# A macaron layer on one core: four products summed by one instruction a step, and attention's weights inverted on 128 partitions by way of DRAM

## The chip, the cores and the metric

The kernel runs on one core of a Trainium2 chip. The metric is the device time of one execution in microseconds (us). TensorE (PE), VectorE (DVE), ScalarE (ACT) and GpSimd (POOL) compute; SyncE (SP) and POOL issue the DMAs here. Each engine works through its own list in order and waits on semaphores, so a wait holds up everything behind it on that engine.

## What is computed

Everything is float32. The input is 4 batches of 512 tokens of width 512. A layer is feed-forward, attention, feed-forward, each added to the stream after a row normalisation:

```
x = x + 0.5 * ffn(layernorm(x))
x = x + attention(layernorm(x))
x = x + 0.5 * ffn(layernorm(x))
ffn: top 2 of 8 experts (512 -> 256 -> 512, gelu) + a shared pair 512 -> 512 -> 512
attention (K=32 heads, H=8 columns, M=8 frequencies):
  z = causal conv of 4 taps over x @ W_mem;  q = x @ W_q
  p = exp(log weight), one row of 512 per head
  num(t) = cumsum over t of p * cos(k*theta_m), p * sin(k*theta_m)
  den(t) = cumsum of p;  out = sum over m of num * q / max(den, 1e-4)
  gated by silu, then @ W_out
```

The kernel scans `run(t) = run(t-1) * p(t-1)/p(t) + cos` (and the same with sin), which is num(t)/p(t); so it needs the **falls** p(t-1)/p(t) inside the scan and the **fractions** p(t)/den(t) afterwards.

## The kernel before, in words

All five lists are written out at build time by a planner. `piece(engine, stage, cost, *after)` declares a stage with an assumed duration and what it comes after; `orders()` then fills each engine in turn with the open piece of longest remaining way. Attention's vector pieces are put behind all others that are open. So a changed cost or dependency moves pieces on every engine, far from the edited code.

**Feed-forward.** Jobs q = 0 to 7 (batches 0 to 3, twice). A job loads rows (`fetch`), normalises, turns them (L710), computes logits (L719), the shared hidden layer (L736) and its second product (L748), added to DRAM by POOL. Two jobs make a group g; its token pairs are sorted by expert into 23 blocks, each: rows gathered by POOL (L1538), turned (L780), two products with the expert's weights (L789, L805), and one accumulating scatter (L1551). The 23 scatters of a group run one after another, because each may hit rows of the one before.

**Attention.** It starts for batches 0 and 1 when group 0 is done, for 2 and 3 when group 1 is done. Per batch: three conv inputs and four query products on PE (L824, L833), queries stored to DRAM (`q_cols<-xin`, L1689), the convolution and log weights on DVE, the exponential on ACT (L1030). Then DVE works out falls and fractions on the 32 partitions that hold one head each: `falls` (L1304, L1306) and `denominators` (L1312 to L1318). PE spreads falls to 128 partitions by a product with 0/1 rows (L840) and ACT keeps the result in `pwx` (L1037); PE spreads the fractions (L846) when they are used.

Then 16 **steps** per batch, 64 in all: 2 halves of the heads by 8 frequencies m. A step loads its queries into `qx` (SP, L1704, two DMAs), makes phases (DVE, L1330 and L1332), cos and sin (ACT, L1043 to L1046), scans (L1343, twice), multiplies real and imaginary parts (L1350, L1355), and adds: two instructions join the two halves of each product (L1366, L1368), and from m = 1 on two more add these to `outT` (L1374, L1376). `trig` and `qx` have two slots, so a step's phases and queries wait for the sums of the step before last. After 8 steps `scale_output` (L1388) multiplies by the fractions, SP moves the result to `outT` (L1710), PE, ACT and DVE apply the gate (L858, L1056, L1400), PE makes the output rows (L867) and POOL adds them to the stream. Only then can the second feed-forward job of that batch fetch its rows.

Of the kernel before, what the change touches and what calls it, by code (L numbers as in the profile page):

```python
# [15 lines left out]
P = 128  # L16
# [45 lines left out]
def macaron(nc, x, small, gate_w, sw1, sw2, b2_rows, w_experts, w_mem, w_q, w_bd, w_out, out):  # L62
# [32 lines left out]
    with ctx:  # L95
# [13 lines left out]
        pw, logw_sb = (low_rows[0:K, :, :], low_rows[2 * K:3 * K, :, :]), low_rows[K:2 * K, 0, :]  # L109
        w_all = sb("w_all", [P, E * WE])  # L110
# [55 lines left out]
        cmp_a = sb("cmp_a", [P, TB, E, E])  # L166
        cmp_b = sb("cmp_b", [P, TB, E, E])
# [20 lines left out]
        past = cmp_a.rearrange("p t e f -> p (t e f)")[:, 0:NB * E].rearrange("p (j e) -> p j e", e=E)  # L188
        is_of = cmp_b.rearrange("p t e f -> p (t e f)")[:, 0:NB * E].rearrange("p (j e) -> p j e", e=E)
        of_bias = past  # L190
# [5 lines left out]
        NK = 2 * HALVES  # L196
        kval = sb("kval", [P, NK, T])
        pwx = sb("pwx", [P, HALVES, T])
        outT = sb("outT", [P, HALVES, 2, T])
        NQX = 2  # L200
        qx = sb("qx", [P, NQX, 2, T])

        trig = sb("trig", [P, 2, 2, T])
        trig_int = trig.bitcast(I32)
        run = sb("run", [P, 2, T])[:, :, :]
# [26 lines left out]
        q_dram = nc.dram_tensor("q_cols", (2, KQ, M, HH, 2, T), F32)  # L232
        slots_dram = [nc.dram_tensor(f"slots{g}", (P * NB, 2), F32).ap() for g in range(NG)]
# [141 lines left out]
        def plan_head(b):  # L375
# [14 lines left out]
            for i in (HALVES, *range(HALVES)):  # L390
                s = ("a_mem", b, i)
                free = [("DVE", ("c_turn", b - 2, i * M + M - 1))] if i < HALVES and b >= 2 else []
                free += [("DVE", ("a_den", b - 1))] if i == HALVES and b else []
# [4 lines left out]
                  *([("PE", ("c_out", b - 2, HALVES - 1)), ("PE", ("a_spread", b - 2, HALVES - 1))] if b >= 2 else []))  # L398
# [8 lines left out]
            for half in range(HALVES):  # L407
                s = ("a_spread", b, half)
                piece("PE", s, 1.2, ("DVE", ("a_fall", b)),
                      *([("DVE", ("c_scan", b - 1, half * M + M - 1))] if b else []), bank=[("misc", ("ACT", s))])  # L410
                piece("ACT", s, 0.6, ("PE", s))

        def plan_step(i):
# [6 lines left out]
            piece("DVE", ("c_scan", b, n), 2.5, ("ACT", ("c_turn", b, n)), ("ACT", ("a_spread", b, half)),  # L420
# [489 lines left out]
        def scalar_program():  # L910
# [121 lines left out]
            def keep_falls(b, half):  # L1032
                bank = misc_turn.at["a_spread", b, half][0]
                act.wait_ge(*spread_p.at((b, half)))
                if b > 0:
                    act.wait_ge(*scanned.at((b - 1, half * M + M - 1)))
# [827 lines left out]
```

## Time and profile before

| | |
|---|---|
| median of 3 runs | 1300.2 us (1297.55 to 1307.3) |
| the profiled execution: its own time, its span | 1298.54 us, 1297.3 us |
| mean granted TensorE clock | 0.894 of full speed |
| busy: PE, DVE, ACT, POOL | 1018.4, 718.9, 586.2, 447.5 us |
| DMA issued on SP, on POOL | 93.58 MB, 60.90 MB |

No engine is busy throughout, and the shares are averages over stages. Up to 243 us DVE has almost nothing to do (expert group 0); from 290 to 1031 us it is busy 80% of the time with attention, beside the expert groups 1 and 2; after 1031 us it is idle again. Durations of DVE instructions in these rows overlap by up to 0.08 us where one does not depend on the other, so a sum of busy time is not the time that a sequence takes: the distance between two starts is.

### The profile page before, as it was taken

What the parts mean: (1) busy time and instruction counts of PE and PEld (TensorE: products, weight loads), DVE (VectorE), ACT (ScalarE), POOL (GpSimd) and SP (SyncE); (2) the same over time, 40 slices, a digit from 0 to 9 for tenths busy, and PEclk for the clock granted to TensorE, in tenths of its full rate; (3) what the DMA queues carried; (4) which work ended last, traced back from release to release, by engine and by line L of the source; (5) the groups of instructions that cost most, each with busy time, mean ns of one, the idle gap of its engine ahead of it and who ended that gap; (6) DMA issues with size and microseconds to landing.
All of it is one profiled execution on the core that took longest, in us unless ns stands there. A gap on an engine that the chain in (4) does not pass through costs nothing.

```text
span 1297.3 us, 10733 instructions
## 1 busy us (share of the span) xinstructions
PE 1018.4 (78%) x3296; PEld 562.8 (43%) x3296; DVE 718.9 (55%) x1162; ACT 586.2 (45%) x1003; POOL 447.5 (34%) x428
## 2 busy tenths in 40 slices
PE   6999779972969869969946379877976897979884
PEld 3547545422525435445412144344443543546552
DVE  4311000077779979979998978889977810200000
ACT  4324333323415768567423254268475741214332
POOL 4164443202453343332000227144354212244442
PEclk9999998995878979988987779889988999789888
DMA  8955554424154656675333742367775525035554
GB/s 299 373 155 97 99 89 74 78 61 137 27 105 109 165 118 138 134 211 148 83 99 77 198 113 51 81 177 147 147 209 121 80 36 108 30 73 96 94 92 53
DMA packets 60204, 155.15 MB, mean 120 GB/s; under 512 B 10578, under 2 KB 10578, under 8 KB 57974
## 3 DMA queue, kind: packets, MB, share of 16 engines
q0 software_dynamic: 29568, 60.90, 27.7%
q1 hardware_dynamic: 30582, 93.58, 23.9%
q8 instruction: 28, 0.46, 0.2%
q14 instruction: 26, 0.21, 0.1%
HBM read 99.74 MB, written 58.88 MB: 122 GB/s over the span
## 4 chain that ended last, share of the span: by engine, by line
DMA 37%; PE 25%; DVE 15%; POOL 8%; ACT 7%; issue 7%; SPq 1%; POOLq 0%; ACTq 0%; DVEq 0%
DMA out_rows<-ys,into_i 14%; DMA x_rows<-ys,into_i 12%; PE hps L736 5%; POOL slots L1526 4%; PE misc L867 4%; DMA xs<-x_normal,rows_i 3%; PE yps L748 3%; DVE run L1343 3%; DMA xin<-x_rows 2%; PE yps L805 2%; PE xps L719 2%; ACT ys L975 2%; PE hps L789 2%; PE misc L833 2%; DVE trig L1350 1%
## 5 line engine op out<-in xcount | busy, mean ns | idle before, releaser
L805 PE MATMUL yps<-w_all,hidden_sb 128*128 x368 | 194.5, 656 | 47.8 <-ACT hidden_sb L962 47.2
L789 PE MATMUL hps<-w_all,hidden_sb 128*128 x736 | 182.4, 393 | 4.0 <-ACT hidden_sb L945 4.0
L789 PEld LDWEIGHTS hps<-w_all,hidden_sb 128*128 128x128 f32 x736 | 143.0, 200 | 47.8 <-issue 31.2
L1343 DVE TENSOR_TENSOR_SCAN run<-pwx,trig 128x512 f32<-128x512 f32 x128 | 149.4, 1208 | 24.0 <-ACT trig L1046 23.4
L1538 POOL DMA_INDIRECT xs<-x_normal,rows_i x92 | 106.9, 1162 | 109.3 <-PE xps L780 82.1
L1551 POOL DMA_INDIRECT x_rows<-ys,into_i x46 | 82.7, 1797 | 158.3 <-DMA x_rows<-ys,into_i 84.9
L736 PE MATMUL hps<-xnT,sw_sb 128*128 128x512 f32 x256 | 130.8, 666 | 7.5 <-ACT hidden_sb L935 6.8
L975 ACT ACTIVATE ys<-yps,slots 128x512 f32<-128x512 f32 x92 | 62.9, 685 | 160.5 <-DMA out_rows<-ys,into_i 61.6
L1551 POOL DMA_INDIRECT out_rows<-ys,into_i x46 | 81.0, 1761 | 152.3 <-DMA out_rows<-ys,into_i 76.3
L805 PEld LDWEIGHTS yps<-w_all,hidden_sb 128*128 128x128 f32 x368 | 70.4, 203 | 117.5 <-issue 115.6
L748 PE MATMUL yps<-sw_sb,hidden_sb 128*128 128x512 f32 x256 | 118.4, 605 | 0.0
L780 PE MATMUL xps<-ident,xs 128*128 128x128 f32 x368 | 58.2, 288 | 69.3 <-DMA xs<-x_normal,rows_i 66.9
L1526 POOL DMA_INDIRECT slots<-told,dest_i x64 | 74.3, 1161 | 72.3 <-DVE cmp_a L1213 30.8
L867 PE MATMUL misc<-turns_sb,tail_sb 128*128 128x512 f32 x192 | 88.6, 615 | 7.6 <-DVE tail_sb L1404 7.6
L710 PE MATMUL xps<-ident,xin 128*128 128x128 f32 x128 | 26.1, 360 | 76.7 <-ACT xin L996 71.1
L736 PEld LDWEIGHTS hps<-xnT,sw_sb 128*128 128x128 f32 x256 | 53.7, 215 | 73.8 <-issue 66.1
L780 PEld LDWEIGHTS xps<-ident,xs 128*128 128x128 f32 x368 | 44.2, 146 | 87.1 <-DMA xs<-x_normal,rows_i 63.2
L1259 DVE BATCH_NORM_STATS2 stats_attn<-xin 128x6 f32<-128x512 f32 x16 | 10.5, 688 | 127.7 <-DMA xin<-x_rows 127.6
L1350 DVE TENSOR_TENSOR trig<-run,qx 128x1024 f32<-128x1024 f32 x64 | 77.9, 1218 | 4.0 <-DMA qx<-q_cols 3.6
L1355 DVE TENSOR_TENSOR qx<-run,qx 128x1024 f32<-128x1024 f32 x64 | 77.9, 1217 | 0.0
L1043 ACT ACTIVATE trig<-trig 128x512 f32<-128x512 f32 x64 | 40.4, 631 | 74.1 <-DVE trig L1332 74.0
L748 PEld LDWEIGHTS yps<-sw_sb,hidden_sb 128*128 128x128 f32 x256 | 46.0, 189 | 53.7 <-issue 53.7
(193 smaller groups left out, 1570.8 us busy)
## 6 DMA issues: line engine op xcount, KB each, us to landing
qx<-q_cols SPq DMA_DIRECT2D x128, 256.0 KB
x_normal<-xin SPq DMA_DIRECT2D x32, 256.0 KB, 3.2
w_all<-in_w_experts SPq DMA_DIRECT2D x8, 1024.0 KB, 9.0
xin<-x_rows SPq DMA_DIRECT2D x32, 256.0 KB, 6.6
turns_sb<-in_w_out SPq DMA_DIRECT2D x3, 1536.0 KB, 10.4
xin<-in_x SPq DMA_DIRECT2D x16, 256.0 KB, 3.6
x_rows<-ys POOLq DMA_DIRECT2D x16, 256.0 KB, 4.6
q_cols<-xin SPq DMA_DIRECT2D x16, 256.0 KB
```

The lines of the kernel that those rows point to most:

```text
L736: t = PE.matmul(hps[:, bank, :], sw1_sb[:, c, n * P:(n + 1) * P], xnT[:, c, :], start=c == 0, stop=c == KC - 1)
L748: t = PE.matmul(yps[:, bank, :], hT[:, n, tb * P:(tb + 1) * P], sw2_sb[:, n, :], start=False, stop=n == SC - 1)
L780: t = PE.transpose(xps[:, bank, c * P:(c + 1) * P], xs[:, j % NX, c * P:(c + 1) * P], ident[:, :])
L789: t = PE.matmul(hps[:, bank, 0:H], xT[:, j % 2, c, :], w_all[:, bass.ds(expert[j] + c * H, H)], start=c == 0, stop=c == KC - 1)
L805: t = PE.matmul(yps[:, bank, :], hb[:, j % 2, ec, :], w_all[:, bass.ds(expert[j] + (KC * H + ec * D), D)], start=ec == 0, stop=ec == EC - 1)
L867: t = PE.matmul(misc[:, bank, :], yT[:, v, tb * P:(tb + 1) * P], wout_sb[:, v, :], start=v == 0, stop=v == VT - 1)
L975: SE.activation(ys[:, j % 2, :], yps[:, bank, :], ACT.Copy, scale=slots[:, g % 2, j, 1:2]).then_inc(*ys_kept.of((g, j)))
L1343: t = VE.tensor_tensor_scan(run[:, c, :], pwx[:, n // M, :], trig[:, n % 2, c, :], 0.0, ALU.mult, ALU.add)
L1350: VE.tensor_tensor(trig[:, n % 2, :, :], run[:, :, :], qx[:, n % NQX, :, :], ALU.mult).then_inc(*real_made.of((b, n)))
L1526: GE.indirect_dma_start(slots_dram[g], bass.IndirectOffsetOnAxis(dest_i[:, g % 2, t, r:r + 1], 0), told[:, g % 2, t, r, :], None).then_inc ...
L1538: GE.indirect_dma_start(xs[:, j % NX, :], None, xn_rows[g % 2], bass.IndirectOffsetOnAxis(rows_i[:, g % 2, j:j + 1], 0)).then_inc(*xs_load ...
L1551: GE.indirect_dma_start(INTO[g], bass.IndirectOffsetOnAxis(into_i[:, g % 2, j:j + 1], 0), ys[:, j % 2, :], None, compute_op=ALU.add).then_ ...
```

## The change

**Sums.** One tile `sums` [128, 2, 2, 512] holds all four sums (two products for the real and two for the imaginary part). `trig` and `qx` become two planes of one tile `steps_sb`, so one instruction over 2048 elements adds all four products. A step with m = 0 writes its products straight into `sums`, and must wait until the previous half has been scaled. The two halves of each part are joined once per half, after m = 7. `outT` loses its dimension for the half; the number of kept conv tiles falls from 4 to 3; `cmp_a` and `cmp_b` shrink.

**Weights.** p is stored to DRAM (one element into the tensor) and read back twice as 128 rows of 128, once as it is and once shifted by one: reciprocal and product then run over 128 elements instead of 512. Falls go to DRAM and are read back with each row repeated 8 times, straight into `pwx`: no product on PE and no copy on ACT. The running sum of p stays on 32 partitions, goes to DRAM, comes back as 128 x 128, and the fractions return the same way. Per batch that is ten DMAs on SP's queue. The planner's costs and dependencies follow.

```diff
-            piece("DVE", ("a_fall", b), 4.0, ("ACT", ("a_p", b)))
-            piece("DVE", ("a_den", b), 5.8, ("DVE", ("a_fall", b)))
+            piece("SP", ("a_p", b, 0), 0.5, ("ACT", ("a_p", b)))
+            piece("SP", ("a_p", b, 1), 0.9, ("SP", ("a_p", b, 0), 2.4), *([("DVE", ("a_frac", b - 1))] if b else []))
+            piece("DVE", ("a_fall", b), 1.4, ("SP", ("a_p", b, 1), 2.4))
+            piece("SP", ("a_den", b, 1), 0.5, ("SP", ("a_den", b, 0), 2.4))
+            piece("DVE", ("a_frac", b), 1.8, ("SP", ("a_den", b, 1), 2.4), ("SP", ("a_p", b, 1), 2.4))
...
-            piece("DVE", ("c_sum", b, n), 2.8 if m else 1.4, ("DVE", ("c_times", b, n)),
-                  *([] if m or not b else [("PE", ("o_gate", b - 1, half * VH + VH - 1))]))
+            piece("DVE", ("c_sum", b, n), 0.1 if m == 0 else 2.4 if m < M - 1 else 3.8, ("DVE", ("c_times", b, n)))
...
             def falls(b):
-                p, fall = pw[b % 2][:, 0, :], pw[b % 2][:, 1, :]
-                vec.wait_ge(*p_made.at(b))
-                VE.reciprocal(fall, p).then_inc(*falling.of((b, 0)))
+                vec.wait_ge(*u_loaded.at((b, 1)))
+                VE.reciprocal(den_q, u_q).then_inc(*falling.of((b, 0)))
                 vec.wait_ge(*falling.at((b, 0)))
-                VE.tensor_tensor(fall[:, 1:T], p[:, 0:T - 1], fall[:, 1:T], ALU.mult).then_inc(*falling.of((b, 1)))
+                VE.tensor_tensor(fall_q, fall_q, den_q, ALU.mult).then_inc(*falling.of((b, 1)))
...
+            def sum_products(b, n):
+                vec.wait_ge(*real_made.at((b, n)))
+                vec.wait_ge(*imag_made.at((b, n)))
+                if n % M > 1:
+                    vec.wait_ge(*summed.at((b, n - 1)))
+                VE.tensor_tensor(sums[:, :, :, :], sums[:, :, :, :], steps_sb[:, :, n % 2, :, :],
+                                 ALU.add).then_inc(*summed.of((b, n)))
...
+            def move_sums(b, part):
+                if part == 0:
+                    sp.wait_ge(*den_made.at(b))
+                    SP.dma_start(whole_rows(den_dram[b % 2]), s_row).then_inc(*den_stored.of(b))
+                else:
+                    sp.wait_ge(*den_stored.at(b))
+                    sp.wait_ge(*falling.at((b, 1)))
+                    SP.dma_start(den_q, quarters(den_dram[b % 2])).then_inc(*den_loaded.of(b))
```

**How the lists move, at three places.** SP, batch 0, from the first query store on. Before (`qx` are the step's queries, the L1661 rows fetch the next job):

```order
L1689 DMA q_cols<-xin 2x64x512 [waits s_qT] x2
L1704 DMA qx<-q_cols 64x1x1024 [waits s_q_stored1,s_q_stored0]
L1704 DMA qx<-q_cols 64x1x1024 x3
L1689 DMA q_cols<-xin 2x64x512 [waits s_qT] x2
L1661 DMA xin<-in_x 128x512 x2
```

Now (`weights` is p in DRAM, `quarter_rows` the tile of 128 x 128 pieces; the four L1784 rows are the same query loads):

```order
L1784 DMA steps_sb<-q_cols 64x1x1024 [waits s_q_stored1,s_q_stored0]
L1784 DMA steps_sb<-q_cols 64x1x1024
L1725 DMA weights<-low_rows 32x512 [waits s_p]
L1784 DMA steps_sb<-q_cols 64x1x1024 x2
L1732 DMA quarter_rows<-weights 128x128 [waits s_before_first,s_u_stored]
L1733 DMA quarter_rows<-weights 128x128
L1756 DMA sums<-low_rows 32x512 [waits s_den]
L1716 DMA q_cols<-xin 2x64x512 [waits s_qT]
L1760 DMA quarter_rows<-sums 128x128 [waits s_falling,s_den_stored]
L1740 DMA falls<-quarter_rows 128x128
L1749 DMA pwx<-falls 128x1x512 [waits s_falls_stored]
```

The exponential's store stands behind the wait for two query stores, and the third query store stands ahead of the falls' store.

DVE, batch 1, around the falls and fractions. Before (the L1274 and L1277 rows are the convolution of the next tile):

```order
L1355 TENSOR_TENSOR qx<-run,qx 128x1024
L1304 RECIPROCAL low_rows<-low_rows 32x512 [waits s_p]
L1306 TENSOR_TENSOR low_rows<-low_rows 32x511 [waits s_falling]
L1274 TENSOR_SCALAR kval<-misc,small_sb 128x512 [waits s_mem]
L1277 SCALAR_TENSOR_TENSOR kval<-misc,small_sb,kval 128x511 [waits s_convolved]
L1277 SCALAR_TENSOR_TENSOR kval<-misc,small_sb,kval 128x510 [waits s_convolved]
L1277 SCALAR_TENSOR_TENSOR kval<-misc,small_sb,kval 128x509 [waits s_convolved]
L1312 SCALAR_TENSOR_TENSOR low_rows<-low_rows,zero 32x512
L1314 TENSOR_SCALAR low_rows<-low_rows 32x512 [waits s_den]
L1316 RECIPROCAL low_rows<-low_rows 32x512 [waits s_den]
```

Now:

```order
L1337 SCALAR_TENSOR_TENSOR low_rows<-low_rows,zero 32x512 [waits s_p]
L1368 SCALAR_TENSOR_TENSOR run<-pwx,steps_sb 128x512 [waits s_imag,s_trig]
L1368 SCALAR_TENSOR_TENSOR run<-pwx,steps_sb 128x512
L1391 TENSOR_TENSOR sums<-sums,steps_sb 128x2048 [waits s_real]
L1329 RECIPROCAL quarter_rows<-quarter_rows 128x128 [waits s_falls_stored,s_u_loaded]
L1331 TENSOR_TENSOR quarter_rows<-quarter_rows 128x128 [waits s_falling]
L1342 TENSOR_SCALAR quarter_rows<-quarter_rows 128x128 [waits s_den_loaded]
```

The load that L1342 waits for is issued by SP only after L1331 has ended (the wait on `falling` in `move_sums`), and nothing stands between the two.

PE, from the end of expert group 2 to the turning of the last job's rows. Before (L867 are the output rows of batch 3, six instructions each; L748 the shared product of job 6):

```order
L867 MATMUL misc<-turns_sb,tail_sb 128x512 x6
L746 MATMUL yps<-bias_parts 128x512
L748 MATMUL yps<-sw_sb,hidden_sb 128x512 x4
L867 MATMUL misc<-turns_sb,tail_sb 128x512 x6
L746 MATMUL yps<-bias_parts 128x512
L748 MATMUL yps<-sw_sb,hidden_sb 128x512 x4
L710 MATMUL xps<-ident,xin 128x128 x16
```

Now, the end of the blocks (L846 is a block's second product, L893 a gate product, its first pair here that of batch 3's second half; L751 turns a tile of rows):

```order
L893 MATMUL misc<-outT,wbd_sb 128x512
L893 MATMUL xps<-outT,wbd_sb 128x512
L846 ISA
L846 MATMUL yps<-w_all,hidden_sb 128x512
L846 ISA
L846 MATMUL yps<-w_all,hidden_sb 128x512
```

and the same place as before, the end of the output rows (L902; L789 is the shared product, L751 the turning):

```order
L902 MATMUL misc<-turns_sb,tail_sb 128x512 x6
L787 MATMUL yps<-bias_parts 128x512
L789 MATMUL yps<-sw_sb,hidden_sb 128x512 x4
L787 MATMUL yps<-bias_parts 128x512
L789 MATMUL yps<-sw_sb,hidden_sb 128x512 x4
L787 MATMUL yps<-bias_parts 128x512
L789 MATMUL yps<-sw_sb,hidden_sb 128x512 x4
L787 MATMUL yps<-bias_parts 128x512
L789 MATMUL yps<-sw_sb,hidden_sb 128x512 x4
L751 MATMUL xps<-ident,xin 128x128 x16
```

The first gate pair of batch 3's second half now stands ahead of the last block's product, where it stood behind the logits, and all four shared products of job 6 stand behind the last output rows, where three of them stood ahead of these.

## Rows read from the trace of the kernel before

**Rows 1.** Busy time by stretch; columns: stretch, length, PE, PEld, DVE, ACT, POOL, PEclk, DMA share, GB/s.

```profile
1031.00:1090.00 59.00, 59.00 (x159) 27.30 (x158) 8.98 (x32) 20.41 (x25) 8.72 (x9) 0.97 0.40 63
```

**Rows 2.** Groups of DVE instructions by form: busy us, mean ns of one, then idle before.

```profile
L1149 DVE RECIPROCAL gr<-diff 128x4 f32<-128x4 f32 x8 | 1.4, 178 | 0.3
L1199 DVE TENSOR_TENSOR pair<-sel,dest 128x128 f32<-128x128 f32 x4 | 1.2, 292 | 0.1
```

**Rows 3.** DVE in order of time, one step: start us, us, what.

```profile
628.46 1.22 DVE L1355 TENSOR_TENSOR qx<-run,qx 128x1024 f32<-128x1024 f32 x1
629.60 0.68 DVE L1366 TENSOR_TENSOR trig<-trig 128x512 f32<-128x512 f32 x1
...
632.01 2.33 DVE L1343 TENSOR_TENSOR_SCAN run<-pwx,trig 128x512 f32<-128x512 f32 x2
```

**Rows 4.** DVE in order of time, batch 0's weights and first steps.

```profile
275.69 3.33 DVE L1304 RECIPROCAL low_rows<-low_rows 32x512 f32<-32x512 f32 x1
279.06 0.68 DVE L1306 TENSOR_TENSOR low_rows<-low_rows 32x511 f32<-32x511 f32 x1
...
283.97 1.21 DVE L1312 TENSOR_TENSOR_SCAN low_rows<-low_rows,zero 32x512 f32<-32x512 f32 x1
...
289.76 2.34 DVE L1343 TENSOR_TENSOR_SCAN run<-pwx,trig 128x512 f32<-128x512 f32 x2
...
299.34 2.73 DVE L1110 BATCH_NORM_STATS2 stats_ffn<-xin 128x6 f32<-128x512 f32 x4 [3.81 <-DMA xin<-in_x]
...
305.81 1.22 DVE L1350 TENSOR_TENSOR trig<-run,qx 128x1024 f32<-128x1024 f32 x1
```

**Rows 5.** ACT in order of time, batch 0's exponential.

```profile
271.90 0.63 ACT L1030 ACTIVATE low_rows<-low_rows 32x512 f32<-32x512 f32 x1 [0.78 <-DVE low_rows L1297]
```

**Rows 6.** SP's queue in order of time, batch 0: query store, then loads that waited for it.

```profile
269.85 0.54 SPq L1689 DMA_DIRECT2D q_cols<-xin  x1
277.89 2.53 SPq L1704 DMA_DIRECT2D qx<-q_cols  x4
```

**Rows 7.** The tile outT: its moves, SBUF to SBUF, 64 rows of 2 KB.

```profile
DMA to landing us min/median/max: 2.3/2.4/3.3
```

**Rows 8.** Chain of waits in order of time, one such move at 503 us.

```profile
503.29 5.08 DMA outT<-tail_sb
```

**Rows 9.** Page part 6, a load on SP: count, KB each, us to landing.

```profile
xin<-in_x SPq DMA_DIRECT2D x16, 256.0 KB, 3.6
```

**Rows 10.** DVE in order of time, the end of attention's last half.

```profile
1030.24 1.41 DVE L1388 SCALAR_TENSOR_TENSOR tail_sb<-outT,small_sb,misc 128x512 f32<-128x512 f32 x2
```

**Rows 11.** SP's queue in order of time, the four moves behind it.

```profile
1031.68 2.91 SPq L1710 DMA_DIRECT2D outT<-tail_sb  x4
```

**Rows 12.** PE in order of time: last gates, output rows, job 6's shared product, job 7.

```profile
1031.23 3.63 PE L719 MATMUL xps<-gate_sb,xnT 128*128 128x8 f32 x32
...
1045.08 1.02 PE L858 MATMUL misc<-outT,wbd_sb 128*128 128x512 f32 x2
...
1046.80 3.60 PE L736 MATMUL hps<-xnT,sw_sb 128*128 128x512 f32 x8
...
1083.42 5.31 PE L867 MATMUL misc<-turns_sb,tail_sb 128*128 128x512 f32 x12
...
1089.08 3.70 PE L748 MATMUL yps<-sw_sb,hidden_sb 128*128 128x512 f32 x8
1101.71 1.97 PE L710 MATMUL xps<-ident,xin 128*128 128x128 f32 x8 [8.92 <-ACT xin L996]
```

**Rows 13.** POOL in order of time: first and last scatter of groups 2 and 3, 23 each.

```profile
859.02 1.79 POOL L1551 DMA_INDIRECT out_rows<-ys,into_i  x1 [2.73 <-ACT ys L975]
...
1039.90 1.54 POOL L1551 DMA_INDIRECT out_rows<-ys,into_i  x1 [3.79 <-DMA out_rows<-ys,into_i]
...
1168.18 1.63 POOL L1551 DMA_INDIRECT out_rows<-ys,into_i  x1 [2.31 <-ACT ys L975]
...
1292.45 1.55 POOL L1551 DMA_INDIRECT out_rows<-ys,into_i  x1 [3.92 <-DMA out_rows<-ys,into_i]
```

More of the change, by code:

```diff
@@ L109, in macaron @@
         pw, logw_sb = (low_rows[0:K, :, :], low_rows[2 * K:3 * K, :, :]), low_rows[K:2 * K, 0, :]
+        quarter_rows = sb("quarter_rows", [P, 3, T // 4])
+        u_q, fall_q, den_q = [quarter_rows[:, i, :] for i in range(3)]
         w_all = sb("w_all", [P, E * WE])
@@ L232, in macaron, with quarters, whole_rows @@
         q_dram = nc.dram_tensor("q_cols", (2, KQ, M, HH, 2, T), F32)
+        u_dram = [nc.dram_tensor(f"weights{i}", (K * T + 1, 1), F32).ap() for i in range(2)]
+        falls_dram = [nc.dram_tensor(f"falls{i}", (K, T), F32).ap() for i in range(2)]
+        den_dram = [nc.dram_tensor(f"sums{i}", (K, T), F32).ap() for i in range(2)]
+        part_dram = [nc.dram_tensor(f"fractions{i}", (K, T), F32).ap() for i in range(2)]
+        def quarters(dram, start=0):
+            return bass.AP(dram.tensor, dram.offset + start, [[T // 4, P], [1, T // 4]])
+        def whole_rows(dram, start=0):
+            return bass.AP(dram.tensor, dram.offset + start, [[T, K], [1, T]])
         slots_dram = [nc.dram_tensor(f"slots{g}", (P * NB, 2), F32).ap() for g in range(NG)]
@@ L408, in plan_head @@
                 s = ("a_spread", b, half)
-                piece("PE", s, 1.2, ("DVE", ("a_fall", b)),
-                      *([("DVE", ("c_scan", b - 1, half * M + M - 1))] if b else []), bank=[("misc", ("ACT", s))])
-                piece("ACT", s, 0.6, ("PE", s))
+                piece("SP", s, 0.5, ("SP", ("a_fall", b), 2.4),
+                      *([("DVE", ("c_scan", b - 1, half * M + M - 1))] if b else []))
         def plan_step(i):
@@ L1347, in real_products @@
             def real_products(b, n):
+                into = trig[:, n % 2, :, :] if n % M else sums[:, 0, :, :]
                 vec.wait_ge(*scanned.at((b, n)))
                 vec.wait_ge(*q_loaded[n % NQX].at((b, n, QH - 1)))
-                VE.tensor_tensor(trig[:, n % 2, :, :], run[:, :, :], qx[:, n % NQX, :, :],
-                                 ALU.mult).then_inc(*real_made.of((b, n)))
+                if n % M == 0 and STEPS_OF.index((b, n)) >= M:
+                    vec.wait_ge(*out_scaled.at(half_before(b, n)))
@@ L1468, in vector_program @@
                     denominators(*at)
+                elif stage == "a_frac":
+                    fractions(*at)
                 elif stage == "c_turn":
@@ new lines, in store_falls, with spread_falls @@
+            def store_falls(b):
+                sp.wait_ge(*falling.at((b, 1)))
+                if b >= 2:
+                    for half in range(HALVES):
+                        sp.wait_ge(*falls_loaded[half].at(b - 2))
+                SP.dma_start(quarters(falls_dram[b % 2]), fall_q).then_inc(*falls_stored.of(b))
+            def spread_falls(b, half):
+                sp.wait_ge(*falls_stored.at(b))
+                if b > 0:
+                    sp.wait_ge(*scanned.at((b - 1, half * M + M - 1)))
+                src = bass.AP(falls_dram[b % 2].tensor, falls_dram[b % 2].offset + half * KT * T,
+                              [[T, KT], [0, HH], [1, T]])
+                SP.dma_start(pwx[:, half, :], src).then_inc(*falls_loaded[half].of(b))
@@ L1757, in sync_program @@
                         SP.dma_start(x1_rows[i][GR:GR + P, :], xs[:, i, :]).then_inc(*cleared.of(NG + 2 * i + 1))
+                    for i in range(2):
+                        SP.dma_start(u_dram[i][0:1, :], xs[0:1, i, 0:1]).then_inc(*before_first.of(i))
                 elif stage == "w_head":
```

213 lines of the change are left out of this document (123 added, 90 removed).

## The prediction

> **What bounds the kernel now.** I read the busy shares first, then the chain of waits, then DVE, PE and SP in order of time. Three stretches follow one another. Up to 243 us the expert blocks of group 0 run alone; the change adds a few DMAs there and nothing else. From 290 to 1031 us DVE works through 64 steps of attention and is never long without work. From there to 1090 us PE is busy for all of 59.00 us [rows 1]: logits and hidden layer of job 6, gates and output rows of batch 3, job 6's shared products. After 8.92 us of idleness it turns job 7's rows at 1101.71 us [rows 12]; then come job 7 and the last 23 scatters, the last at 1292.45 us [rows 13]. The change touches nothing after 1101.71 us, so its worth is how much earlier that turning starts. Two things hold it: the end of attention's last scaling, at 1030.24 + 1.41 = 1031.65 us [rows 10], and the end of group 2's blocks on PE, at about 1031.2 us, where the logits start [rows 12].
>
> **From these two ends to the end of the kernel.** By the new PE list the first gate pair comes 5.3 us after the last scaling (2.91 us of issues [rows 11], 2.4 us to land [rows 7]). Behind it: three gate pairs of 1.7 (1046.80 - 1045.08), a block's product and a turn, 2.5 (an estimate from such instructions' 0.5 us each, half of the 1.02 a pair), four hidden tiles of 3.5, logits 3.5, four output rows of 5.2, a small turn 0.5, four shared products of 4.1 (3.70 and the bias product ahead of it) [rows 12]. That is 5.3 + 5.1 + 2.5 + 14.0 + 3.5 + 20.8 + 0.5 + 16.4 = 68.1 us after the scaling, 1099.7 us if it did not move: **2.0 us gained by order alone**, since the shared products now cover the time in which job 7's rows are fetched and normalised (13 us from the last output row to the turning, less than the 16.4). If attention is not the last, PE goes on from the blocks' end with two gate pairs, 0.5, 14.0, 3.5, 20.8, 0.5 and 16.4: 59.1 us, or 1090.3 us, so **at most 11.4 us** unless the blocks end earlier too.
>
> **Sums.** Four additions take from 629.60 to 632.01 us, 2.41 us, though each lasts 0.68 [rows 3]: they do not depend on one another and overlap. From 512 to 1024 elements an instruction grows from 0.68 to 1.22 us, so 2048 should last 0.68 + 3 x 0.535 = 2.29. But it waits for the product just before it, which ends at 628.46 + 1.22 = 629.68, and a dependent instruction starts 0.04 later (279.06 behind 275.69 + 3.33 [rows 4]); it would end at 632.01, and the next start 0.08 earlier: 0.08 a step, not 0.45. Times 56: 4.5 us. The m = 0 steps lose two additions (8 x 1.2 = 9.6), the joining after m = 7 adds two and a dependence (8 x 1.32 = 10.6). **Net 3.5 us**; between 0 and 11, the latter if another piece stands between product and sum each time. The new wait of a m = 0 step on the scaling stands right behind it in DVE's own list and costs nothing while that one does not wait.
>
> A rule speaks for more. The Trainium skill ("VectorE: DVE Perf Modes", The DRAIN you can't avoid) says that the next operation does not start before the pipe is empty and that only the count of operations matters; by it each of the 56 steps gives 0.45 us, 25 in all. The starts in [rows 3] lie 2.41 apart over four operations of 0.68, so this trace does not agree.
>
> **Weights on DVE.** Before, a batch spends 4.05 us on falls (3.33, one product of 0.68, 0.04) and 289.76 - 283.97 = 5.79 on sums and fractions [rows 3, 4]. A reciprocal grows from 0.178 us at 4 elements to 3.33 at 512 [rows 2, 4], 6.2 ns an element, so 0.95 at 128; other operations on 128 x 128 take 0.29 [rows 2]. Falls: 0.95 + 0.29 + 0.08 = 1.32; running sum 1.25; fractions 0.29 + 0.95 + 0.29 + 0.12 = 1.65. 4.2 for 9.8: **5.6 us a batch** before waits. PE's two small products and ACT's two copies a batch go too; neither engine is waited for there, so I put that at nothing.
>
> **Waits.** The falls now need a store and two loads after the exponential, on SP about 0.55 + 2.4 + 1.1 + 2.4 = 6.5 us at the landing of [rows 7], and a store and a load of 256 KB, 3.0 + 4.2 [rows 7, 9], before the scan. Nothing of this is in the trace of before; a landing lies between 2.4 [rows 7] and 5.1 us [rows 8]. I take 2.4, the same size of move, but later where a query store is ahead: one issued at 269.85 lets the loads behind it go only at 277.89, so it takes 7.5 us [rows 6]. The Trainium skill ("DMA: Bandwidth & Descriptors", Rules for kernel authors) says that an outermost dimension below 16 confines a DMA to that many engines, and this store's is 2; a small transfer on 16 engines would then wait behind it on two.
>
> - Batch 0. The exponential is done at 272.5 [rows 5], but the store waits for SP until 279.1 (two query loads after 277.89). Loads land at 286.5, falls end at 287.8, their store lands with the third query store at 292, the spread load at 296. The first scan starts 6.4 us later than 289.76. But phases and fractions are then done, two scans and products follow at once, and before, DVE stood 3.81 us for job 3's rows [rows 4]; the second step's products come at about 304.7 instead of 305.81. **Gain 1.1**, between -6 and 5.
> - Batch 1. The wait for the exponential stays. Behind it a query store goes out just ahead of the loads, so they land 9.5 us after the exponential, with 5.8 us of work in between: 4 us of wait. The load for the fractions is issued only after the falls and follows at once in DVE's list: 0.5 + 2.4 = 2.9. **5.6 - 6.9 = -1.3**, between -10 and 3.
> - Batches 2 and 3 have 8 us of other work ahead of the falls and 3 to 5 ahead of the fractions; I leave 1 us of wait: **4.6 each**, between -4 and 5.6.
>
> **The sum.** Attention's end: 3.5 + 1.1 - 1.3 + 9.2 = 12.5 us earlier, which by order gives 14.5. Group 2 starts after batch 1's output rows, so its blocks end earlier only by half the sums and the first two batches: 1.7 + 1.1 - 1.3 = 1.5, which gives 11.4 + 1.5 = **12.9**, the smaller. 1298.5 - 12.9 = 1285.6 us for the profiled execution; that one lies 1.7 us below the median of the runs shown, so **1287 us**.
>
> **Rivals.** A measurement of this kernel tells about 1% (13 us) from no change: its three runs lie 10 us apart.
> - *As forecast*, 1281 to 1292 us: 0.37, on both sides of 1% (1287), 0.23 of it faster.
> - *The blocks shorten too*, 1272 us: group 2's 22 gaps between scatters take (1039.90 - 859.02) / 22 = 8.2 us, group 3's, alone, 5.65 [rows 13]. Attention's pieces now stand earlier among the blocks. If a quarter of that 56 us goes, 14 more, less what attention then lacks. For: DVE is 12 us ahead. Against: the blocks wait for ACT, PE and DMA in turn. 0.22.
> - *Joined sums at their full 0.45 us*: attention 33 us earlier, blocks 12, so 1298.5 - 23.5, 1277 us by the median. 0.04; it is the rule above.
> - *The gain stops at the blocks*: batch 1 loses more than it gains, the blocks end 5 us later, 11.4 - 5 = 6.4 left: 1294 us. For: all waits priced at the quiet landing. 0.22.
> - *Slower: SP's list becomes the wait.* Each batch's ten DMAs stand in one list with the queries' loads, and six are followed by a wait for landing. At 5.1 us a landing (2.7 more each for store, load, store, spread) and a query store of 7.5 ahead, a batch loses up to 18 us of start, of which cover takes half. In three batches it eats the 20.3 us saved and the 2.0 of order from 7.4 us each; at 12 each it makes the kernel 13.7 slower: 1314 us. For: the 5.1 is from where batch 0 ends. Against: before, query stores already stood in that list ahead of loads [rows 6], and DVE kept its pace. 0.13.
> - *The wide addition does not do it*: were 2048 elements slower than twice a 1024 one (2.44), 8 us go: 1295 us. 0.02.
>
> Faster by over 1%: 0.23 + 0.22 + 0.04 = 0.49. Within 1%: 0.14 + 0.22 + 0.02 = 0.38. Slower: 0.13. The range, 1264 to 1307 us, takes in the blocks' rival with half as much again and the milder half of the slower one.
>
> **What the new trace would show.** The 2048 additions at 2.3 us, starting 0.04 after the product; DVE busy down by about 49 us (25 for sums, 23 for weights), four times what attention gains. The first scan near 296 us. In batch 1 a wait on u of about 4 and on the sums of about 3 us. The last scaling near 1019 us, the blocks' end near 1030, and PE without the gap of 8.92 us before job 7. I am wrong if a query load makes DVE wait, if the fractions' wait exceeds 5 us, or if the end of the blocks moves by over 8 us either way.

## The result and the profile after

The changed kernel is **slower: 1339.5 us** (median of four, 1326.6 to 1348.9) against 1303.6; the ratio is 1.026, 95% interval [1.021, 1.031]. I had forecast 1287 us and a range to 1307. The profiled execution (1348.88 us, span 1347.6) is the slowest of the four and counts as a slow run, which the ratio leaves out. Its span is 50.3 us over that of before, where the ratio says 34 us, so lengths read from it overstate the loss. 8.6 us of it are lost at the start: the rows of batch 0's attention arrive at 248.59 us, against 240.00 before; in `move_first` below, the same kernel but for the place of one load in SP's list, they arrive at 237.73. Further kernels are compared by ratio to the kernel before on the same chip, since chips differ by up to 9 us.

On the whole page VectorE was busy for 718.9 us before, and is for 689.7 now:

```profile
PE 1029.4 (76%) x3280; PEld 570.2 (42%) x3280; DVE 689.7 (51%) x994; ACT 584.6 (43%) x997; POOL 462.7 (34%) x428
...
L1391 DVE TENSOR_TENSOR sums<-sums,steps_sb 128x2048 f32<-128x2048 f32 x56 | 128.2, 2289 | 4.2
```

So VectorE did get its work off, and the wide addition lasts what was forecast. Now from the first scan to the last scaling, VectorE alone (stretch, length, busy, TensorE clock, DMA share, GB/s); before the same stretch was 742.60 us with 644.83 busy:

```profile
307.01:1068.63 761.62, 620.29 (x735) 0.84 0.52 124
```

24.5 us less work, 19.0 us more time: the waits in it grew from 97.8 to 141.3 us. The attention's end moved by 36.3 us: 8.6 from the early part, 8.6 from the later first scan, 19.0 here. The same stretch of `move_first`, profiled in an execution of 1330.8 us, has the same work and is 14 us shorter, 5.0 us longer than before:

```profile
298.81:1046.44 747.63, 620.73 (x735) 0.86 0.54 127
```

Which waits (`after`, VectorE between 285 and 1100 us; total, times, longest):

```profile
DVE tail_sb L1424 <- ACT tail_sb L1082: 52.1, 8, 16.8
DVE run L1368 <- ACT steps_sb L1072: 20.5, 10, 5.8
DVE quarter_rows L1329 <- DMA quarter_rows<-weights: 20.3, 3, 10.3
DVE quarter_rows L1342 <- DMA quarter_rows<-sums: 11.0, 4, 4.4
DVE steps_sb L1379 <- DMA steps_sb<-q_cols: 10.9, 3, 5.2
```

31.3 us are the weights' own round trips. The first row, 25.0 us before, is the multiplications with the output gates. This window reaches past both ends of the stretch. Its longest wait for the gates, 16.77 us, comes behind the last scaling, and 10.27 us of the wait on the weights come ahead of the first scan:

```profile
1084.69 0.69 DVE L1424 TENSOR_TENSOR tail_sb<-misc,tail_sb 128x512 f32<-128x512 f32 x1 [16.77 <-ACT tail_sb L1082]
```

Inside the stretch the gates' row reads, before and now:

```profile
DVE tail_sb L1400 <- ACT tail_sb L1056: 15.7, 6, 6.9
```

```profile
DVE tail_sb L1424 <- ACT tail_sb L1082: 31.8, 6, 16.6
```

That is 16.1 us more. The weights' loads add 20.3 there (10.1 and 10.2), and the waits for query loads go from 3.6 to 10.9: the three make 43.7 us, about the 43.5 by which the waits grew, and the smaller rows nearly cancel. The largest piece of the gates' row inside the stretch is at the end of batch 1. SP in order of time there:

```profile
689.22 0.53 SPq L1804 DMA_DIRECT2D turns_sb<-in_w_out  x1
689.80 0.57 SPq L1716 DMA_DIRECT2D q_cols<-xin  x1
690.42 1.35 SPq L1749 DMA_DIRECT2D pwx<-falls  x1
691.88 3.44 SPq L1767 DMA_DIRECT2D fractions<-quarter_rows  x1
707.23 0.33 SPq L1772 DMA_DIRECT2D low_rows<-fractions  x1
707.60 1.23 SPq L1784 DMA_DIRECT2D steps_sb<-q_cols  x2
708.93 2.45 SPq L1792 DMA_DIRECT2D outT<-tail_sb  x4
```

The fractions are stored behind a query store and 1.5 MB of weights, and the next entry of the list waits for them. By the issues' own view this store of 64 KB took 15.3 us to land (another, of the running sums, issued right behind a query store in batch 3, took 9.5). Taken one at a time in that view, the eight small stores that SP issues within 3 us of a query store landed after 7.4 to 15.3 us, the other eight after 2.4 to 7.2:

```profile
fractions<-quarter_rows SPq DMA_DIRECT2D x1, 64.0 KB, 15.3
...
sums<-low_rows SPq DMA_DIRECT2D x1, 64.0 KB, 9.5
```

outT's moves, which need nothing of this, stand behind it. VectorE, with the scaling done and its next entries waiting for the gates:

```profile
694.56 1.40 DVE L1412 SCALAR_TENSOR_TENSOR tail_sb<-sums,small_sb,misc 128x512 f32<-128x512 f32 x2
...
702.73 2.34 DVE L1368 TENSOR_TENSOR_SCAN run<-pwx,steps_sb 128x512 f32<-128x512 f32 x2
721.69 0.69 DVE L1424 TENSOR_TENSOR tail_sb<-misc,tail_sb 128x512 f32<-128x512 f32 x1 [16.62 <-ACT tail_sb L1082]
```

TensorE waits there too, but it did before (21.00 us at 688.23, the first row here), so only some 3 us of its wait are new:

```profile
688.23 2.05 PE L858 MATMUL misc<-outT,wbd_sb 128*128 128x512 f32 x2 [21.00 <-DMA outT<-tail_sb]
```

```profile
689.62 3.70 PE L789 MATMUL yps<-sw_sb,hidden_sb 128*128 128x512 f32 x8
717.27 2.05 PE L893 MATMUL misc<-outT,wbd_sb 128*128 128x512 f32 x2 [23.95 <-DMA outT<-tail_sb]
```

The end, in the order of [rows 10 to 13]: last scaling, last block product of group 2, turning of job 7, last scatter.

```profile
1066.52 1.41 DVE L1412 SCALAR_TENSOR_TENSOR tail_sb<-sums,small_sb,misc 128x512 f32<-128x512 f32 x2
```

```profile
1082.89 1.98 PE L846 MATMUL yps<-w_all,hidden_sb 128*128 x4 [1.04 <-ACT ys L1008]
...
1149.54 1.27 PE L751 MATMUL xps<-ident,xin 128*128 128x128 f32 x8 [1.89 <-ACT xin L1029]
```

```profile
1342.84 1.55 POOL L1578 DMA_INDIRECT out_rows<-ys,into_i  x1 [3.94 <-DMA out_rows<-ys,into_i]
```

Scaling + 36, blocks' end + 54 (1084.9), turning + 48, last scatter + 50. From the blocks' end to the turning it took 64.7 us, where I had 59.1 for that case; the 8.92 us of idleness ahead of job 7 did shrink, to 1.89.

### The profile page after: what moved, and what is told of

Same layout as the page of the kernel before. It is cut to its first block and busy times, and to the rows that moved or that the text cites. A ratio compares the mean times of both kernels' runs of the same rounds, so it can differ in the third digit from the quotient of the medians.

```text
span 1347.6 us, 10625 instructions
## 1 busy us (share of the span) xinstructions
PE 1029.4 (76%) x3280; PEld 570.2 (42%) x3280; DVE 689.7 (51%) x994; ACT 584.6 (43%) x997; POOL 462.7 (34%) x428
## 5 line engine op out<-in xcount | busy, mean ns | idle before, releaser
L846 PE MATMUL yps<-w_all,hidden_sb 128*128 x368 | 195.1, 657 | 47.5 <-ACT hidden_sb L995 43.4
L830 PE MATMUL hps<-w_all,hidden_sb 128*128 x736 | 188.9, 404 | 22.5 <-ACT hidden_sb L978 18.3
L830 PEld LDWEIGHTS hps<-w_all,hidden_sb 128*128 128x128 f32 x736 | 147.1, 206 | 64.0 <-issue 45.4
L1368 DVE TENSOR_TENSOR_SCAN run<-pwx,steps_sb 128x512 f32<-128x512 f32 x128 | 149.3, 1207 | 23.0 <-ACT steps_sb L1072 20.5
L1565 POOL DMA_INDIRECT xs<-x_normal,rows_i x92 | 110.2, 1198 | 95.2 <-PE xps L821 70.7
L1391 DVE TENSOR_TENSOR sums<-sums,steps_sb 128x2048 f32<-128x2048 f32 x56 | 128.2, 2289 | 4.2
L846 PEld LDWEIGHTS yps<-w_all,hidden_sb 128*128 128x128 f32 x368 | 70.7, 205 | 120.4 <-issue 118.8
L789 PE MATMUL yps<-sw_sb,hidden_sb 128*128 128x512 f32 x256 | 120.8, 615 | 0.0
L821 PE MATMUL xps<-ident,xs 128*128 128x128 f32 x368 | 61.7, 299 | 68.1 <-DMA xs<-x_normal,rows_i 62.9
L1553 POOL DMA_INDIRECT slots<-told,dest_i x64 | 77.2, 1206 | 65.8 <-DVE cmp_a L1237 35.9
L902 PE MATMUL misc<-turns_sb,tail_sb 128*128 128x512 f32 x192 | 88.4, 614 | 7.1 <-DVE tail_sb L1428 7.1
L1069 ACT ACTIVATE steps_sb<-steps_sb 128x512 f32<-128x512 f32 x64 | 40.3, 630 | 113.7 <-DVE steps_sb L1357 113.7
L751 PE MATMUL xps<-ident,xin 128*128 128x128 f32 x128 | 25.1, 343 | 83.5 <-ACT xin L1029 77.3
L1379 DVE TENSOR_TENSOR steps_sb<-run,steps_sb 128x1024 f32<-128x1024 f32 x56 | 68.3, 1219 | 11.2 <-DMA steps_sb<-q_cols 10.9
L789 PEld LDWEIGHTS yps<-sw_sb,hidden_sb 128*128 128x128 f32 x256 | 46.9, 193 | 55.8 <-issue 55.8
```

The lines of the kernel that those rows point to most:

```text
L789: t = PE.matmul(yps[:, bank, :], hT[:, n, tb * P:(tb + 1) * P], sw2_sb[:, n, :], start=False, stop=n == SC - 1)
L821: t = PE.transpose(xps[:, bank, c * P:(c + 1) * P], xs[:, j % NX, c * P:(c + 1) * P], ident[:, :])
L830: t = PE.matmul(hps[:, bank, 0:H], xT[:, j % 2, c, :], w_all[:, bass.ds(expert[j] + c * H, H)], start=c == 0, stop=c == KC - 1)
L846: t = PE.matmul(yps[:, bank, :], hb[:, j % 2, ec, :], w_all[:, bass.ds(expert[j] + (KC * H + ec * D), D)], start=ec == 0, stop=ec == EC - 1)
L902: t = PE.matmul(misc[:, bank, :], yT[:, v, tb * P:(tb + 1) * P], wout_sb[:, v, :], start=v == 0, stop=v == VT - 1)
L1368: t = VE.tensor_tensor_scan(run[:, c, :], pwx[:, n // M, :], trig[:, n % 2, c, :], 0.0, ALU.mult, ALU.add)
```

## The experiments

All ratios are to the kernel before, with 95% intervals.

**One half at a time.** The two halves of the change share few lines; `sums_only` keeps the hunks on the sums, outT, kval and c_sum's costs, `weights_only` the others.

```diff
 sums_only (three of its lines)
+NK = 3
+outT = sb("outT", [P, 2, T])
+sums = sb("sums", [P, 2, 2, T])
 weights_only (two of its lines)
+quarter_rows = sb("quarter_rows", [P, 3, T // 4])
+u_q, fall_q, den_q = [quarter_rows[:, i, :] for i in range(3)]
```

> Half of the change alone: the joined sums with their single outT, three kval tiles and the planner's new costs for the sums; attention's weights stay on 32 partitions and in PE's list as before. Theory A (the loss comes from the weights' way through DRAM, whose waits stand in SP's list in front of other transfers): the sums are a small gain by themselves, attention's last scaling 1 to 6 us earlier than in the kernel before, time 1290 to 1303. Rival B (the loss comes with the sums: one outT, whose moves wait for the gates of the half before, and one kval tile fewer): 1320 to 1340, with the long wait of VectorE for ScalarE's gates at the end of batch 1 as in the changed kernel. Rival C (neither; the list that the planner writes is what moved): anything between 1290 and 1330, and not the sum of the two halves.

> The other half alone: the weights on 128 partitions by way of DRAM, falls spread by DMA; sums in four adds, two outT tiles and four kval tiles as before. Theory A: 1320 to 1345, with waits of SP for the fractions' store of about 10 us at the end of batch 1 and what stands behind it late. Rival B: 1290 to 1305, since the weights save 5.6 us of VectorE per batch and outT has both halves. Rival C: between the two.

Measured: sums 1.006 [1.002, 1.009], weights 0.999 [0.995, 1.002]. Theory A and rival B both fall: neither half has the loss. Together they have 2.6%, where the two add up to 0.4. The sums' 1312.0 us lies between theory A's 1290 to 1303 and rival B's 1320 to 1340, the weights' 1301.8 in the range of rival B, by which the sums should have had the loss. What came is rival C's "not the sum of the two halves". From the first scan to the last scaling VectorE's work falls by 6.7 us with the sums alone (638.18 against 644.83) and by 17.8 with the weights alone (627.00), while the stretch goes from 742.60 to 750.17 and 738.31.

**SP's list**, and **the planned order of the kernel before.**

```diff
 move_first, behind the planner
+for b in range(1, B):
+    names = ORDERS["SP"]
+    load, move = ("a_frac", b, 1), ("c_out", b - 1, HALVES - 1)
+    if names.index(move) > names.index(load):
+        names.remove(load)
+        names.insert(names.index(move) + 1, load)
 before_costs
-piece("DVE", ("c_sum", b, n), 2.8 if m else 1.4,
+piece("DVE", ("c_sum", b, n), 0.1 if m == 0 else 2.4 if m < M - 1 else 3.8,
```

> The changed kernel with one reordering of SP's list: the load of the fractions of batches 1 to 3 is issued behind the moves of outT of the batch before, where it stood ahead of them. In the changed kernel SP waited 11.9 us for the fractions' store at 695 us, outT's moves were issued 13 us after the scaling had ended, and VectorE then waited 16.6 us for the gates. Theory A: that wait goes, attention ends 10 to 16 us earlier, time 1322 to 1332 against 1339.5. Rival B (outT's moves are late for another reason, or the wait comes back at the next place): 1335 to 1343.

> The kernel before with nothing changed but three numbers of the planner: the sums of a step are planned at 0.1, 2.4 and 3.8 us (first, middle and last step of a half) in place of 1.4 and 2.8. All instructions are the same, only their order in the lists may move. Theory A: the order alone is worth little, 1295 to 1310. Rival C (the kernel is sensitive to the planned order, and the change lost its gain there): 1315 or more.

Measured: 1.021 [1.017, 1.025] and 0.992 [0.989, 0.995]. The place in front of outT's moves is worth 0.5%, 6 us of the 36, with intervals that overlap; 1333 us lies between the two theories. At the end of batch 1 outT's moves now leave 1.05 us after the scaling in place of 12.97, and VectorE's wait there is 9.79 us in place of 16.62. It is not the main thing. Three numbers of the planner, with no instruction changed, gave 0.8% on the kernel before. That is more than either half of the change did, so each comparison below in which the planner's costs or dependencies differ carries such a term. Splitting the query stores changes none of them.

**Who blocks the small stores?** Two suspects stand ahead of them: the large reloads, and the query stores, which took 7.5 us in [rows 6].

```diff
 bulk_act, bulk_act_before: w_out, w_mem, w_q, out_rows<-x_rows
-SP.dma_start(wout_sb, w_out).then_inc(*tail_loaded.of(b))
+SE.dma_start(wout_sb, w_out).then_inc(*tail_loaded.of(b))
 qsplit: [[T, 2], [2 * T, 64], [1, T]] becomes two of [[2 * T, 64], [1, T]]
-SP.dma_start(bass.AP(q_dram, (b % 2 * KQ + q) * P * T, [[T, 2], [2 * T, M * HH], [1, T]]),
-             xin[:, q, :]).then_inc(*q_stored[q].of(b))
+for i in range(2):
+    SP.dma_start(bass.AP(q_dram, (b % 2 * KQ + q) * P * T + i * T, [[2 * T, M * HH], [1, T]]),
+                 xin[i * M * HH:(i + 1) * M * HH, q, :]).then_inc(*q_stored[q].of((b, i)))
 landings
-piece("SP", ("a_frac", b, 1), 0.5, ("SP", ("a_frac", b, 0), 2.4))
+piece("SP", ("a_frac", b, 1), 0.5, ("SP", ("a_frac", b, 0), 9.0))      (and seven more)
```

> The changed kernel with its large transfers on ScalarE's DMA queue: the reloads of w_out (1.5 MB, three times), of w_mem and w_q (1.6 MB, twice) and the copies of x_rows into out_rows (four) are issued from ScalarE's list, at the places where what they wait for has just ended; SP's list keeps its order without them. Theory D (small transfers that stand behind a large one on SP's queue land late: in the changed kernel the fractions' store landed after 15 us behind w_out's 1.5 MB, outT's moves after up to 12.8 us, 64 KB stores after 4 to 9 us where I had counted 3.3): outT's slowest landing falls from 12.8 to under 6 us, the 16.6 us wait of VectorE for the gates near 700 us goes, time 1315 to 1328. Rival E (the queue is innocent; the lists' order and SP's own waits are it): 1333 to 1345. A third way: the large transfers slow the small ones on either queue, since the 16 engines are shared; then landings stay above 8 us and the time within 5 us of 1339.

> The kernel before with the same move of the large transfers to ScalarE's queue. Its outT moves landed in 2.3 to 3.3 us, so nothing critical stood behind the large transfers: theory D and rival E both say within 8 us of 1303.9, either side. If it gained as much as the changed kernel does, the queue would be no part of the difference between the two.

> The changed kernel with each store of a query tile (256 KB, its outermost dimension 2, landing after 7.5 us in the kernel before) written as two stores of 64 rows. Two of the four stores of a batch stand right in front of a small store of the weights. Theory D: the stores land in 4 us, the small one behind them in 4 where it took 8 to 9; the chain from the weights' exponentials to the fractions is 4 to 8 us shorter in each batch, time 3 to 10 us less than the changed kernel's 1339.5. Rival E: within 3 us of it. If the two dimensions were no limit, the landings stay.

> The changed kernel, its planner told the landings that the trace of it shows, where it had 2.4 us for each: 5.0 for the weights' store, 4.5 for their load, 5.5 for the falls' store, 7.5 for the sums' store, 3.0 for their load, 9.0 for the fractions' store, 3.0 for their load, 4.3 for outT's moves. Same instructions, another order. Rival E (order): VectorE's waits on these loads, 31 us in all between 290 and 1070 us, fall to under 15, and the time to 1318 to 1330. Theory D: the transfers are as late as before and only what stands around them moves: 1328 to 1345.

Measured: bulk_act 1.035 [1.029, 1.040], bulk_act_before 1.001 [0.998, 1.005], **qsplit 1.009 [1.006, 1.013]**, landings 1.018 [1.012, 1.024]. bulk_act lies above all three of its ranges, bulk_act_before where both theories had it. landings came into rival E's time (1318 to 1330), but the waits on the weights' loads, 25.1 us, did not fall under 15. Theory D was right about small stores behind something, and only in one place about the large transfers: at the end of batch 1, with 1.5 MB no longer ahead, the fractions' store landed in 7.9 us in place of 15.3 and VectorE's wait for the gates fell from 16.62 to 9.02 us. Elsewhere the fractions still land late, and VectorE waits longer for the sums' load than in the change (20.9 us against 11.0). The edit also put the waits of these transfers into ScalarE's list and moved their times, so its own 0.9% (intervals just overlap) is not a measure of the queue alone. The fractions' issues and the waits on the sums:

```profile
fractions<-quarter_rows SPq DMA_DIRECT2D x4, 64.0 KB, 8.2
```

```profile
DVE quarter_rows L1365 <- DMA quarter_rows<-sums: 20.9, 4, 9.2
```

With the query stores split, the same rows, and those stores themselves:

```profile
q_cols<-xin SPq DMA_DIRECT2D x32, 128.0 KB, 2.4
...
fractions<-quarter_rows SPq DMA_DIRECT2D x4, 64.0 KB, 4.6
```

```profile
DVE tail_sb L1424 <- ACT tail_sb L1082: 47.4, 9, 17.5
...
DVE quarter_rows L1342 <- DMA quarter_rows<-sums: 7.0, 2, 3.9
DVE quarter_rows L1329 <- DMA quarter_rows<-weights: 6.9, 3, 5.3
```

The fractions' median landing of 9.1 us became 4.6, the waits on the round trips 13.9 us where they were 31.3, and the kernel 1.7% faster, 22 us by the ratios and far more than the 3 to 10 us that I gave it. The weights' store hardly moved (4.9 to 4.7), and at the end of batch 1, where 1.5 MB still go ahead, the fractions' store took 8.0 us in place of 15.3. The Trainium skill ("DMA: Bandwidth & Descriptors", Rules for kernel authors) says that an outermost dimension below 16 confines a transfer to that many engines. The landings agree; but the split also makes two transfers of one, and no view here shows how many engines a transfer used, so that this is the reason is not shown.

**Is it the change's loss, or any kernel's gain?** The same split in the kernel before and in each half; and the split change with its planner told 4.0, 3.0, 4.0, 4.0, 3.0, 4.6, 3.0 us.

> The kernel before with each store of a query tile as two stores of 64 rows. It has no small stores of the weights; behind a query store stand only query loads, which are early. Theory F (the changed kernel loses because its small stores, and what waits for them in SP's list, stand behind the 7.5 us stores of the query tiles): 1298 to 1305, a gain of at most 5 us, so that nearly all of the 25 us that the split gave the changed kernel belong to the change. Rival G (the split helps any kernel alike, by freeing the queue and the xin tile): 1275 to 1285.

> The weights by way of DRAM alone (1301.8 without the split; sums, outT and kval as before), with the query stores split. Theory F: the small stores land in 4 us in place of up to 8, in four batches; 5 to 15 us less, 1287 to 1297, below the kernel before. Rival G: as much as the kernel before gains by the split.

> The joined sums alone (1312.0 without the split), with the query stores split. No small stores: theory F says 1306 to 1312. Rival G: 1287 or so.

> The changed kernel with the query stores split (1314.3) and the planner told of landings as they are then: 4.0, 3.0, 4.0, 4.0, 3.0, 4.6 and 3.0 us in place of 2.4, 3.3 for outT's moves. If the order written from landings that are too short is the rest of the loss (told the landings, the unsplit kernel came from 1339.5 to 1325.8), this comes to 1298 to 1308. If the rest is the sums' (1312 alone against 1303.9), it stays at 1310 to 1316.

| | unsplit | split | gain of the split |
|---|---|---|---|
| before | 1 | 0.996 [0.992, 0.999] | 0.4% |
| sums alone | 1.006 | 1.001 [0.998, 1.004] | 0.5% |
| weights alone | 0.999 | **0.980 [0.974, 0.986]** | 1.9% |
| the change | 1.026 | 1.009 [1.006, 1.013] | 1.7% |
| the change, landings told | 1.018 | 1.000 [0.998, 1.003] | 1.8% |

Theory F holds in kind: kernels that put small stores behind the query stores get 1.7 to 1.9%, the others 0.4 to 0.5%. In size it was low for the weights, 24 us where it had 5 to 15. So about 1.3% of the change's 2.6%, some 17 us, is what the split gives beyond its gain in the kernel before (0.6 to 2.0% by the intervals), and the weights alone, freed of it, beat both kernels. It does not explain why joining the halves costs: the change lies above the sum of its halves by 2.2% without the split (1.026 against 1.004) and by 2.8% with it (1.009 against 0.981). The stretch from first scan to last scaling there:

```profile
289.61:1004.80 715.19, 625.65 (x903) 0.87 0.56 134
```

with the first scan where it was before the change, and batch 0's wait on the weights down from 10.27 us (in the change and in the weights alone) to

```profile
282.80 0.95 DVE L1314 RECIPROCAL quarter_rows<-quarter_rows 128x128 f32<-128x128 f32 x1 [5.28 <-DMA quarter_rows<-weights]
```

**What the halves lose when joined.** All with split stores.

```diff
 w_costs: weights alone, c_sum planned at 0.1 / 2.4 / 3.8;   c_oldcosts: the change, at 1.4 / 2.8
 w_narrow: weights alone (and the planner's two dependencies for it)
-NK = 2 * HALVES
+NK = 3
+if half or b:
+    sp.wait_ge(*y_made.at((b, VH - 1) if half else (b - 1, VT - 1)))
 w_landings: weights alone, landings told;   winner: qsplit_weights again;   qsplit_first: qsplit and move_first
```

> The weights by way of DRAM alone with the query stores split (0.980 of the kernel before), its planner told the sums' costs of the change, 0.1, 2.4 and 3.8 us in place of 1.4 and 2.8. No instruction changes, only the order of the lists. Theory H (what the two halves lose when joined is the planned order): 0.99 to 1.005 of the kernel before. Theory I (it is the storage that the joined sums need, one outT and three kval tiles, or the sums themselves): 0.975 to 0.985.

> The same kernel of weights and split stores, with the storage limits of the joined sums and nothing else of them: three kval tiles, and outT's moves wait for the gates of the half before as if there were one outT; four adds a step as before. Theory I: 0.995 to 1.01. Theory H: between 0.975 and 0.99, unless the planner's new dependencies move the order too.

> The changed kernel with split query stores (1.009 of the kernel before), its planner told the old costs of the sums, 1.4 and 2.8 us. Again the order alone. Theory H: the time changes by more than 1%, most likely down to 0.985 to 1.0. Theory I: it stays at 1.005 to 1.013.

> The kernel of weights and split stores (0.980), its planner told landings of 4.0, 3.0, 4.0, 4.0, 3.0, 4.6 and 3.0 us in place of 2.4, as the joined kernel was (1.009 to 1.000). If honest landings help wherever there are small transfers: 0.970 to 0.978. If they only moved that one order by luck: 0.978 to 0.99.

> The changed kernel with split query stores and the fractions' load behind outT's moves in SP's list, both edits at once. In the split kernel (1.009) outT's moves at the end of batch 1 were still issued 6 us after the scaling, behind the wait for the fractions' store, and VectorE waited 10.5 us for the gates. If the two losses add: 1.003 to 1.006. If the rest is the joined kernel's planned order alone: 1.008 to 1.010.

> The kernel of weights by way of DRAM and split query stores once more, in five rounds: every theory says what it measured before, 0.974 to 0.986 of the kernel before.

Measured: w_costs 0.988 [0.982, 0.994], w_narrow 0.985 [0.979, 0.992], c_oldcosts 1.002 [0.998, 1.006], w_landings 0.991 [0.987, 0.995], **qsplit_first 1.000 [0.997, 1.004]**, **winner 0.981 [0.977, 0.986]**. Of the five kernels that tried something, w_narrow's 0.985 speaks against theory I (0.995 to 1.01); w_costs and c_oldcosts fall between H and I, w_landings just outside both of its ranges, and qsplit_first beat its 1.003 to 1.006. The order alone moves the weights' kernel by 0.8% and the joined one by 0.7%, both faster with the old costs, while the kernel before was faster with the new ones; telling the true landings helped the joined kernel by 0.8 to 0.9% and hurt the weights' by 1.1%, so it drew another order, not reliably a better one. In the joined kernels the other orders share one thing. At the end of batch 1 outT's moves leave 5.8 us after the scaling in qsplit (1.009) and within 0.03 us of it in qsplit_first (1.000), qsplit_landings (1.000) and c_oldcosts (1.002). Three different edits thus come to the same time with the same place put right; whether the last two do more than that was not separated. The storage costs 0.5%, with overlapping intervals: not told apart. qsplit_first says that two edits on transfers, and none on arithmetic, undo the whole loss; the kernel before with the split is at 0.996.

Between 1.000 and 0.981 something of the joined kernel stays open. In every joined kernel I profiled VectorE's waits for ScalarE's gates and waves between 285 and 1100 us sum to 69 to 82 us, in the kernel before to 56, in each half alone to 47 to 72. The sum does not order the kernels: weights_only has 72 us at 0.999, landings 69 at 1.018. They move between the two: 47.4 and 25.2 in qsplit, 10.7 and 57.1 in qsplit_landings. Whether that is the single sums tile, which holds a half's first product until the last scaling, or the order, was not tried apart.

## Why the prediction was wrong

- **The step that failed is the landing: "I take 2.4, the same size of move".** I had seen the query store's 7.5 us, cited the rule for it, and charged it to batch 0's spread load and batch 1's wait on u alone. Measured medians of the small stores: 4.9 (weights), 5.4 (falls), 7.7 (sums), 9.1 (fractions), once 15.3. The 64 KB loads behind them did take the quiet 2.2 to 2.4. The weights alone show what it cost: with 22.5 us of VectorE's work gone they stood at 0.999; with the query stores split they are at 0.980.
- **The second error is of place: I priced waits only where VectorE waits for the weights.** SP's list is in order too, and outT's moves, which no part of the weights feeds, stood behind the fractions. My rival "SP's list becomes the wait" had this mechanism, with query stores ahead, at 0.13 and 1314 us, 25 us short of what came. Against it I had held that loads already stood behind query stores without harm. They did, and cost one wait of 3.6 us before: a query load is issued before its step needs it, while VectorE's next entries wait for a round trip.
- **What stays open.** The forecast was 0.987 of the kernel before, the measurement 1.026: 3.9% apart. The split takes back 1.7 and the entry in SP's list 0.9. The other 1.3% stays; the weights alone with split stores (0.980) do not have it, so it comes with joining the halves, and no run shows by what.
- *Of my three signs of being wrong* two came: query loads made VectorE wait 10.9 us in three waits, and the end of the blocks moved by far more than 8 us. The wait for the sums' load stayed under 5 (4.4).
- *First scan at 296*: 307.0, or 298.4 without the early 8.6. Nearly right, 2.4 late.
- *Batch 1 waits 4 and 3*: 4.5 on u and 1.9 on the sums. Right. *Batches 2 and 3 wait 1*: 3.9 on the sums, then 5.6 and 4.4. Wrong by the landings.
- *Sums*: 2.289 us, and the dependent start costs what it should: at the last step the product ends at 1062.67, the addition starts at 1062.76 and ends at 1065.05, within 0.05 of the forecast. Sums alone took 6.7 us of work off; 3.5 were forecast. Right that it is small. The 25 us that I drew from the Trainium skill's section ("VectorE: DVE Perf Modes", The DRAIN you can't avoid) did not come, and I had read only half of it: it adds that a next operation that is not held starts earlier, which is what [rows 3] show. But the term was a gain, and the half measured 0.6% slower.
- *Weights 5.6 a batch*: on the whole page weights_only has VectorE busy for 696.4 us against 718.9, 22.5 less, 5.6 a batch. Right. (The 17.8 above leave out batch 0, whose weights come ahead of the first scan.)
- *VectorE's busy time down by 49*: down by 29.2, which is the 22.5 and the 6.7 of the halves. For the sums I added up durations that overlap; the page counts the time covered.
- *Attention 12.5 earlier*: 27.7 later without the early part. *Blocks 1.5 earlier*: 45 later. Both are read from that longest execution; in `move_first` attention ends 14.1 us later. I had let the blocks gain or lose only through batch 1. Group 2's first scatter comes 36.2 us later (895.26 against 859.02), and its 23 scatters take 203.6 us where they took 180.9. The blocks share PE's list with the gates: among them TensorE now waits once for outT, 8.13 us at 997 us, and did not before. The rest of the 22.7 us was not taken apart.
- *The rival "the blocks shorten too" at 1272* breaks the rule of its own sum, that the later of two ends counts: attention's end gives 14.5 us at most, so it comes to 1286.
- *The gap before job 7 goes*: 8.92 to 1.89. Right.

## What to carry to other kernels

Before adding a chain of small transfers to a queue, look up what is issued just ahead of each: a store that lands late, as the query stores did here, is harmless while only early loads follow it, and becomes the price of each link of the chain. Then ask who else stands behind each new wait in that list, fed or not. And where a planner writes the lists, rerun the old kernel with the new costs: here that alone moved the time by 0.8%, more than either half of the change did.

## What was unexpected of the hardware

A store of 256 KB whose outermost dimension is 2 landed in 7.5 us, and the eight 64 KB stores issued within 3 us of one took 7.4 to 15.3 us. As two stores of 64 rows the parts had medians of 2.4 to 4.4 us in eleven kernels. Moving 1 to 1.6 MB transfers to a second queue freed the one small store that stood right behind such a transfer (15.3 to 7.9 us) and not the others: the fractions' median went from 9.1 to 8.2 us.
